# Mixture-of-experts layers of a token tower: down products of two expert pairs in one group

## The reference, cut to what matters

```python
# block 0
gate_scores = jnp.einsum('bsd,ed->bse', x, Wg) + bg
topk_scores, topk_idx = jax.lax.top_k(gate_scores, K)          # K = 2 of 8
...
for e in range(E):
    h = jax.nn.relu(jnp.einsum('bsd,hd->bsh', x, W1[e]) + b1[e])   # 64 -> 256
    y = jnp.einsum('bsh,dh->bsd', h, W2[e]) + b2[e]                # 256 -> 64
    out = out + combine[..., e:e + 1] * y
# block 1
for e in range(NE):
    hh = jax.nn.silu(flat @ w1[e].T) * (flat @ w3[e].T)            # 64 -> 170
    out = out + weights[:, e:e + 1] * (hh @ w2[e].T)               # 170 -> 64
```

## Time and profile before

| | us |
|---|---|
| median of 3 runs | 1102.91 |
| lowest and highest | 1093.0, 1104.26 |
| the profiled execution | 1097.99 |
| its span, first to last instruction | 1096.2 |
| mean granted PE clock | 0.987 |
| PE busy | 1004.6 (92%) |
| DVE, ACT, POOL busy | 808.0 (74%), 580.6 (53%), 399.7 (36%) |

### The profile page before, as it was taken

The page is one execution under the profiler, slowest core; times in us unless marked ns, Lnnn a source line. Parts: engine busy times, 40 slices in busy tenths (PEclk is TensorE's granted clock), DMA queues, the critical chain, the costliest instruction groups (busy, mean ns, idle before and its releaser), DMA issues. The chain is left out here.

```text
span 1096.2 us, 23392 instructions
## 1 busy us (share of the span) xinstructions
PE 1004.6 (92%) x8389; PEld 720.9 (66%) x8389; DVE 808.0 (74%) x1982; ACT 580.6 (53%) x1331; POOL 399.7 (36%) x391
## 2 busy tenths in 40 slices
PE   5798889879999999998988799988999999999997
PEld 2476766557677767775765577755777777777774
DVE  2595968967766776777777589866877778777775
ACT  2275646565565656564338666765444444444441
POOL 3233602312433343333357568710133333333333
PEclk9899999999999999999999989999999999999999
DMA  8300000003223222322001000000122221221122
GB/s 227 136 2 1 2 2 1 1 12 87 49 51 82 66 50 51 84 63 50 1 19 49 7 2 2 2 3 0 51 65 71 71 65 55 56 55 56 55 56 68
DMA packets 76423, 50.16 MB, mean 46 GB/s; under 512 B 4196, under 2 KB 75124, under 8 KB 75924
## 3 DMA queue, kind: packets, MB, share of 16 engines
q1 hardware_dynamic: 75972, 44.59, 15.8%
q0 software_dynamic: 336, 4.07, 0.9%
HBM read 45.99 MB, written 2.66 MB: 44 GB/s over the span
## 5 line engine op out<-in xcount | busy, mean ns | idle before, releaser
L1579 PE MATMUL moe_psU<-moe_nT_parts,moe_w_hi 128*128 128x320 f32 x988 | 322.6, 338 | 14.1 <-DVE moe_hid L1483 8.8
L1579 PE MATMUL moe_psU<-moe_nT_parts,moe_w_lo 128*128 128x320 f32 x988 | 294.1, 308 | 0.0
L1579 PEld LDWEIGHTS moe_psU<-moe_nT_parts,moe_w_hi 128*128 128x128 f32 x988 | 185.6, 188 | 71.7 <-issue 42.4
L1225 ACT ACTIVATE moe_hid<-moe_psU,middle 128x320 f32<-128x320 f32 x312 | 149.6, 528 | 99.3 <-PE moe_psU L1579 97.7
L1220 ACT ACTIVATE moe_silu<-moe_psU 128x320 f32<-128x320 f32 x286 | 123.9, 439 | 139.2 <-PE moe_psU L1579 112.1
L1579 PEld LDWEIGHTS moe_psU<-moe_nT_parts,moe_w_lo 128*128 128x128 f32 x988 | 186.3, 189 | 0.7 <-issue 0.7
L1483 DVE TENSOR_TENSOR moe_hid<-moe_psU,moe_silu 128x320 f32<-128x320 f32 x286 | 131.3, 485 | 34.4 <-ACT moe_silu L1220 27.6
L1111 POOL TENSOR_TENSOR moe_y_sum<-moe_y_sum,moe_y 128x320 f32<-128x320 f32 x96 | 81.7, 872 | 145.7 <-DVE moe_y L1444 82.1
L1594 PE MATMUL moe_psY<-moe_hid,late 128*64 128x320 f32 x800 | 118.7, 439 | 0.0
L1594 PE MATMUL moe_psY<-moe_hid,middle 128*64 128x320 f32 x800 | 118.6, 439 | 0.0
L139 POOL TENSOR_TENSOR moe_stats<-moe_stats,minus_half 128x5 f32<-128x5 f32 x26 | 30.5, 1171 | 186.3 <-DVE moe_stats L1326 186.3
(11 more groups left out here) (367 smaller groups left out, 1901.3 us busy)
## 6 DMA issues: line engine op xcount, KB each, us to landing
moe_share<-shares SPq DMA_DIRECT2D x208, 160.0 KB, 4.5
images<-in_x SPq DMA_DIRECT2D x8, 576.0 KB, 11.4
late<-in_late POOLq DMA_DIRECT2D x1, 2263.5 KB, 11.3
out_tokens<-h SPq DMA_DIRECT2D x13, 160.0 KB, 1.8
middle<-in_middle POOLq DMA_DIRECT2D x1, 1554.0 KB, 7.1
project_turns<-in_turns SPq DMA_DIRECT2D x8, 160.0 KB, 2.2
early<-in_early SPq DMA_DIRECT2D x1, 1043.0 KB, 18.9
turns_first<-in_turns SPq DMA_DIRECT2D x4, 160.0 KB, 2.3
```

What stands on the lines that cost most here:

```text
L1225: act.activation(hid[hid_of(g, u)][:, :], psU[u % 4][:, 0:HALF], ACT.Relu, bias=late[:, c["b1"]][:, k:k + 1]).then_inc(hid_act, 1)
L1579: last = pe.matmul(psum[:, 0:HALF], w[:, col:col + SPLIT], moving, start=(part == 0), stop=(part == 1))
```

## The change

- Down products run twice a tile, for pairs 0 and 1 behind the place where pair 0's stood, and for pairs 2 and 3 behind pair 2's (`DOWNS`, `down_two`). DVE weighs both pairs at that place.
- `psY` has three banks. An even pair's 640 columns lie at 128 to 768, an odd pair's at 768 to 1408, so each is written in two parts, 384 and 256 columns or the reverse, and the middle bank holds a part of both. The even pair is reported done only after the odd pair's first part. The shares' transpose moves into the third bank, at 1408.
- A hidden buffer holds one chunk for all 640 columns.
- For the bank that `psY` takes, layer 0 gives one of `psM` and so turns tile and output in the parts 4 and 1; layer 1 gives one of the three gate banks.
- In layer 0 DVE empties six of every sixteen units (12 of 32) instead of 8 of 32.
- The routing and norm steps are put elsewhere in `SLOTS`; in layer 0 the shares are transposed behind (3,6) and copied behind (3,7), before behind (2,6) and (2,7).
- The last tile's down products are ordered anew.

```diff
-        on_dve = [(u - first_of[units[u][0]]) in (2, 6) for u in range(UPG)]
+        on_dve = [(u - 5) % 16 in (2, 5, 7, 10, 12, 15) for u in range(UPG)]
...
-        hid = [sb(f"hid{k}", [128, HALF]) for k in range(NHID)]
+        hid = [sb(f"hid{k}", [128, TOK]) for k in range(NHID)]
...
-        psU = [ps(f"psU{k}", 128, HALF) for k in range(4 if layer == 0 else 5)]
-        psY_both = ps("psY", 128, 1024)
-        psM = ps("psM", 128, MBANKS * 512)
+        psU = [ps(f"psU{k}", 128, HALF) for k in range(4)]
+        psY = ps("psY", 128, 1536)
+        EVEN_AT, ODD_AT, SHARES_AT = 128, 768, 1408
+        psM = ps("psM", 128, 512)
...
+        OUTS, READS = [(1, 0), (1, 3)], [(1, 1), (1, 4)]
         if layer == 0:
-            LOGITS, DOWN = (0, 2), 4
-            OUTS, READS = [(1, 0)], [(1, 1)]
-            SHARES, SHARES_READ = (2, 6), (2, 7)
-            TURN, KEEP = [(3, 2)], [(3, 2)]
-            HI, EXP = (1, 5), (2, 3)
+            LOGITS, DOWNS = (0, 2), [(0, 4), (2, 4)]
+            SHARES, SHARES_READ = (3, 6), (3, 7)
+            TURN, KEEP = [(3, 2), (3, 4)], [(3, 2), (3, 4)]
+            HI, EXP = (2, 4), (2, 5)
...
-            SLOTS = {(0, 4): "aaaannnn", (1, 0): "n", (1, 2): "n", (1, 4): "aaaaan", (1, 7): "aa", (2, 1): "aaa", (2, 4): "neeeeee"}
+            SLOTS = {(0, 4): "nnnnnnaaa", (1, 0): "aa", (1, 3): "aa", (1, 6): "a", (2, 4): "naaaaaan",
+                     (2, 7): "ee", (3, 1): "ee", (3, 3): "ee"}
         else:
-            LOGITS, DOWN = (0, 0), 1
+            LOGITS, DOWNS = (0, 0), [(0, 1), (2, 1)]
...
-            SLOTS = {(0, 1): "aaaannn", (0, 4): "ee", (1, 1): "neeeeeee", (1, 4): "eee", (2, 1): "neeeeeee"}
+            SLOTS = {(0, 1): "aaaannneeeeee", (1, 1): "ne", (1, 4): "ee", (2, 1): "neeeeeeeeeee"}
...
-                        if g and k == DOWN:
+                        if g and (p, k) in DOWNS:
                             weigh(g - 1, p)
+                            weigh(g - 1, p + 1)
...
-                        turns = [(psU[u % 2], 0, up_mm), (psU[2 + gate_bank[u]], 1, gate_mm)]
+                        turns = [(psU[u % 2], 0, up_mm), (psU[2 + u % 2], 1, gate_mm)]
...
+                            wait_evicted(pe, g, u - 2)
...
+                def down_two(j, p):
+
+                    need(pe, weighed, j * PAIRS + p)
+                    pe.wait_ge(shares_set, j + 1)
+                    down_ready(j, p + 1)
+                    down_part(j, p, 0)
+                    down_part(j, p, 1)
+                    down_part(j, p + 1, 0).then_inc(down_mm, 1)
+                    down_part(j, p + 1, 1).then_inc(down_mm, 1)
+
+                def down_last(j, p):
+
+                    if p == 3:
+                        pe.wait_ge(weighed, j * PAIRS + 2)
+                    down_ready(j, 3)
+                    down_part(j, p, 0, True)
+                    down_part(j, p, 1, True).then_inc(down_mm, 1)
...
                     pe.wait_ge(routed, g + 1)
-                    need(pe, out_read, (g - 1) * PARTS)
-                    pe.transpose(psM[0:T * E, SHARES_AT:SHARES_AT + B],
+                    need(pe, weighed, g * PAIRS)
+                    pe.transpose(psY[0:T * E, SHARES_AT:SHARES_AT + B],
...
-                down(NT - 1, 0, True)
-                pe.wait_ge(shares_set, NT)
+                down_two(NT - 1, 0)
                 for part in range(PARTS):
                     turn_out(NT - 2, part)
-                for p in range(1, PAIRS):
-                    down(NT - 1, p, True)
+                for p in (2, 3):
+                    down_last(NT - 1, p)
```

More of the change, by code:

```diff
@@ L996, in downs @@
     def downs(p):
[L997 to L1004 removed]
+        for j in range(2):
+            for s in range(2):
+                e = 2 * p + s
+                if layer == 0:
+                    yield s, 2 * e + j, 2 * e + j, j == 0, j == 1
+                else:
+                    yield s, e if j == 0 else E + e // 3, 4 * p + 2 * j + s, j == 0, j == 1
     with ExitStack() as ctx:
@@ L1044, in moe @@
         ident = early[:, ec["ident"]]
-        TURNS = [(0, T)] if layer == 0 else [(0, 4), (4, T)]
+        TURNS = [(0, 4), (4, T)]
         PARTS = len(TURNS)
@@ L1049, in outputs_ps @@
         def outputs_ps(p, last):
-            if last and p % 2:
-                return [psU[half][:, 0:HALF] for half in range(2)]
-            return [psY[:, half, :] for half in range(2)]
+            if last and p == 2:
+                return [(half * HALF, (half + 1) * HALF, psU[half][:, 0:HALF]) for half in range(2)]
+            at, middle = (ODD_AT, 2 * B) if p % 2 and not last or p == 1 else (EVEN_AT, 3 * B)
+            return [(0, middle, psY[:, at:at + middle]), (middle, TOK, psY[:, at + middle:at + TOK])]
         def turned_ps(t, last):
-            if layer == 1 and last and t == T - 1:
+            if last and t == T - 1:
                 return psU[2][:, 0:2 * D]
@@ L1466, in last_outputs @@
                     dve.wait_ge(out_mm, j * PARTS + 1)
-                    first_half = 1 if layer == 1 else 0
-                    turned = [(0, 4, psM[:, 0:8 * D]), (4, T, psU[2][:, 0:2 * D])] if layer == 1 else [(0, T, psM[:, 0:2 * T * D])]
+                    first_half = layer
+                    turned = [(0, 4, psM[:, 0:8 * D]), (4, T, psU[2][:, 0:2 * D])]
                     for side in range(2):
@@ L1561, in up @@
                     moving = nTr[g % 2][:, half * HALF:(half + 1) * HALF]
-                    if u == 0 or layer == 1 and half == 1 and units[u - 1][1] == 0:
-                        pe.wait_ge(nTr_set, g * PARTS + (half + 1 if layer == 1 else 1))
+                    if u == 0 or half == 1 and units[u - 1][1] == 0:
+                        pe.wait_ge(nTr_set, g * PARTS + (half + 1))
                     if first_tile and u == first_of[p]:
```

102 lines of the change are left out of this document (42 added, 60 removed).

## The result

| | before | after |
|---|---|---|
| median of 4 runs, us | 1102.55 | 1140.09 |
| lowest and highest | 1093.0, 1104.26 | 1134.81, 1148.38 |
| the profiled execution | 1097.99 | 1148.38 |
| its span | 1096.2 | 1146.6 |
| mean granted PE clock | 0.987 | 0.966 |

A forecast was written before the change was run, and what follows sets the result against it. PE was taken to bound the kernel, by its own sequence and its waits for PSUM banks. 1098.0 profiled + 6 (layer 0, net of merging) + 2 (layer 1) + 0 (first tiles and tails) = 1106 us, range 1086 to 1121.

The forecast's parts named there:

- The price of the merging: Down products, both layers: a merged group saves 0.35 us per excursion, 0.70 a tile; 48 fewer excursions, -16.8 us.
- Rival 4: Down-product groups: alternating 384 and 256 columns or changing banks costs what the excursion cost; 1121 us, chance 0.06.
- Step 1: Layer 0, PE's sequence: turning tile and output in 4 + 1 parts adds two visits, 0.22 a tile, +2.6 us.
- Step 2: Layer 0, units 5 to 20: late shares delay DVE's eviction of unit 7; unit 11 stalls 1.3 us, run 7.0.
- Rival 2: Layer 0: shares land later than computed, each microsecond costing twelve; 1123 us with 1.4 more, chance 0.18.
- Step 3: Layer 0, units 21 to 4: tile's last part waits for ACT's copy, 0.35 with exposed load; run 6.4 us.
- Step 4: First tiles and tails: layer 0's first tile -1, layer 1's +1, layer 0's tail 0; sum 0 us.
- Layer 1 in steady state: Two gate banks stall 1.5 us a tile, less 0.70 merging and 0.6 old stall: 25.45 against 25.25, +2 us.
- Rival 1: Both layers: excursions are saved and the waits stay away; 1086 us, chance 0.27.
- Rival 3: Long unit runs: ACT's evictions take 0.53 instead of 0.42, each run stalls PE 0.6 more; 1120 us, chance 0.06.

The follow-up runs named there:

- `all_mended`: Changed kernel with unread product only in first tile, shares early, high parts and output's second part moved, statistics early, first-tile steps spread: 1100.27 us, 1.0024 of before.
- experiment 8: Kernel before with only layer 1 changed, but routing and norm steps in layer 1's first tile at their old places: 1102.35 us, 1.0034 of before.
- experiment 7: Changed kernel with unread product only in first tile, layer 0's shares early and its last tile's second-norm statistics at their old places: 1124.65 us, 1.0246 of before.
- experiment 14: Layer 0 as in `all_mended`, layer 1 as before, layer 0's last pair-2 product put ahead of the turned output: 1094.44 us, 0.9959 of before.
- experiment 3: Also called `no_unread`: changed kernel with the unread product only in the first tile, as before the change: 1135.82 us, 1.0327 of before.
- experiment 4: Changed kernel with unread product only in first tile, and layer 0 storing and spreading shares in its first tile alone: 1119.64 us, 1.0201 of before.
- experiment 1: Changed kernel with layer 1 put back as before, so only layer 0 is changed: 1136.11 us, 1.0357 of before.
- `weigh_later`: Changed kernel with unread product only in first tile, layer 0's second pair weighed later, behind evictions of units 7 and 23: 1129.55 us, 1.0307 of before.

## Why the prediction was wrong

**The price of the merging was right.** "A lone group costs 2.50, one behind another 2.15": the merged group measured 4.46, as said, and with the 0.09 ahead of it (423.15 to 423.38) and the 0.10 behind it (427.84 to 428.09) it costs 4.65, against twice 2.50. That is 0.35 per excursion, and `all_mended` has the same. The split into 384 and 256 costs nothing that can be seen: a lone group so split takes the same 2.31. Rival 4 is out.

That `all_mended` gains 0.50 a tile of layer 0 looks like the prediction's 0.70 for the merging less 0.22 for two more visits, 0.48. That match is luck. The prediction also had 0.35 for the wait for the transposes' second part, and this wait, 0.42, still stands in the tile. What makes up for it: between up products the starts lose 0.70 beyond their spacing in a tile of before (355.00 to 376.84) and 0.26 in one of `all_mended` (358.54 to 379.88). By the starts, -0.71 for the merging, +0.22 for the visits, +0.42 for the wait and -0.44 for these delays give the 0.50. The prediction's own sum of a tile, without the stall of the first run, would be 5.44 + 6.4 + 2 x 4.46 = 20.8; the runs take 5.72 (363.00 to 368.72) and 6.70 (373.18 to 379.88), the tile 21.34. Why the small delays are fewer no run separates.

**Step 1 that failed: "what layer 0 pays in PE's own sequence" (+0.22 a tile).** The diff put a product of 512 columns into every tile, and the sum had no term for it. The line stands in the diff; it was read as the first tile's alone. It measured 0.86 in PE's sequence and, by the periods, 0.56 a tile in effect, 6 us over eleven tiles.

**Step 2: the waits in the run of units 5 to 20.** The chain and its sizes held: shares at R + 7.0 and R + 8.6 for 6.8 and 8.4, unit 11 late by 1.16 for 1.3. What failed is that one stall of the middle was taken twelve times. Three of eleven tiles wait 1.9 to 2.9, and behind two of these waits PE runs at half clock for 3.4 us. In each of the three the shares are late at another link of their way (see the last section). Rival 2, the shares coming later, named the right mechanism and had a price for each late microsecond, but none for the clock, and its 1123 is still short. Without shares to wait for, eleven tiles were 14.3 us shorter (262.4 to 248.1), which is more than all that the prediction had for layer 0.

**Step 3: the run of units 21 to 4.** 6.4 was predicted, 7.04 is what it takes in the tile shown; the waits for the transposes' second part (0.42, predicted 0.35) were sized right, the small ones beside it were not there in the sum. The first run, predicted 7.0, takes 7.71 with the unread product's 0.86 in it, so this tile's 23.66 against 22.3 is the unread product and this step, less 0.15.

**Step 4: "first tiles and tails", which came to 0.** Layer 1's first tile costs 5.5, not 1: 2 for the routing steps that have no group over them there (experiment 8), 2.5 for the gate bank, the rest unsettled. The prediction had checked that the list fits under a group of 4.46 and had not asked what happens where there is none. Layer 0's tail costs 5.9, not 0: POOL's queue, behind which the sums of tile 11 wait, was not walked although its input had been moved (experiments 7 and 14), and again the clock doubled the price. The 2.7 ahead of it, in the last tile, belong to the steps above: the same wait for DVE's eviction is among them, 1.81 (526.71), while the wait of 1.18 for ACT stands in both kernels (539.53, before 503.52).

**Layer 1 in steady state was right**: 25.68 for 25.60, predicted 0.2 more. (The prediction's 25.25 is not the period: its 303 us hold eleven periods and the shorter last tile.) The two banks measured 1.68 a tile against the 1.5 of stalls worked out, and the long group with the routing steps under it gives back 1.6 against 1.3: each is 0.2 to 0.3 larger than said, and they cancel. The many short waits are there: PE's weight loads wait 47 times for DVE's product in the changed kernel's layer 1, 15 times before.

Rivals 1 and 3 are out: the waits did not stay away, and PE's long waits in the changed kernel's eleven tiles are for DVE's evictions (11 of them, 15.1 us) and for the last transpose (11, 2.8 us), none for ACT's. Over layer 0's eleven tiles the 26.5 us divide, by the stretches of experiments 3 and 4, into 4.1 for the unread product, 14.3 for shares and their clock, and 8.1 for the waits that are then left, the output's second part above all, less the merging's saving. To these come 2.7 in the last tile, 5.9 in the tail, 5.5 in layer 1's first tile and 1.8 in its others; the other 8.0 of the 50.4 are mainly the clock of code that did not change.

## What to carry to other kernels

When a diff moves a place in a schedule, list everything whose guard names that place, and walk each moved step through its worst tile: the first (no cover yet), the last, and every in-order queue behind its result. A wait that hangs on a DMA and sits ahead of an eviction on the same engine should be priced by its late landings, and by the clock that PE loses behind the long ones, not by the median. A gain that is only a saved excursion is worth having once the tables around it are cut for it: here layer 0's merging made the kernel 3.6% slower (experiment 1) or 0.4% faster (experiment 14), by where a dozen small steps stand and by one guard.

## What the hardware showed that I had not expected

- In the changed kernel's trace PE's waits of 1.0 to 1.8 us in layer 0 left the granted clock at 1.00, while those of 2.21, 2.60, 2.13 and 3.30 had 0.50 behind or under their end, for 3.4 us (259.9 to 263.3) up to 6.8 (550.0 to 556.8), and so had the one of 1.88 (0.50 from 311.1). The wait of 2.86 at 383.99 did not, nor one of 2.54 in `no_unread` (307.66); and in `weigh_later` one of 1.18 (526.46), with shorter ones behind it, had 0.50 from 527.8. So the length of a wait alone does not decide it. Behind the wait of 3.30 a group of 2.32 took 4.54, so it cost another 2.2.
- The first four share DMAs landed between 4.1 and 4.8 after their issue in the earlier trace rows, yet in the changed kernel pair 1's share came 8.6 us behind ACT's copy in one tile and 10.4 in another (429.92 - 421.36, 382.59 - 372.19), with nothing in the program that differs between the two. The issues stand at the same distance from the copy in both; in the late tile the fourth DMA landed 6.4 after its issue, in the other one 4.9. The two other long tiles are late elsewhere: in the one with the wait at 309.65 the first share DMA was issued 2.8 after the copy (298.82 to 301.61) and not 1.64, in the one at 260.27 the third issue took 1.76 and not 0.62, so that the fourth went out at 254.4.
